# The attention loop of a graph kernel: one bfloat16 product turns both ends' types, GpSimd adds the residual rows, and a square root with a reciprocal stands for a power

## The reference

```python
h = relu(layernorm(x))
k, q, v = per-type projections of h (weights and biases chosen by node type)
k_rot, msg = k[src], v[src] turned by a 16x16 matrix per head and edge type
att = (q[dst] * k_rot).sum(-1) * pri[edge_type] / 4
alpha = softmax of att over the edges of one destination
aggr = segment_sum(msg * alpha, dst)
res = per-type projection of gelu(aggr), blended with h by sigmoid(skip)
x = x + layernorm(res) * ln_g[type] + ln_b[type]
x = x + graph_conv(graph_conv(relu(layernorm(x))))
```

## Time and profile before

| what | value |
|---|---|
| median of 3 runs | 2546.35 us (2545.54 to 2549.22) |
| span of the profiled execution, first to last instruction | 2543.6 us |
| time of that execution itself | not given; the median lies 2.75 us above its span |
| attention loop within the span | about 350 to 1349 us |
| mean granted TensorE clock over the span | 0.793 |
| PE, DVE, ACT, POOL busy over the span | 69%, 77%, 52%, 65% |

### The profile page before, as it was taken

The page is one execution under the profiler, slowest core; times in us unless marked ns, Lnnn a source line. Parts: engine busy times, 40 slices in busy tenths (PEclk is TensorE's granted clock), DMA queues, the critical chain, the costliest instruction groups (busy, mean ns, idle before and its releaser), DMA issues. The chain is left out here.

```text
span 2543.6 us, 48846 instructions
## 1 busy us (share of the span) xinstructions
PE 1755.3 (69%) x12706; PEld 1459.1 (57%) x12706; DVE 1955.8 (77%) x6737; ACT 1311.8 (52%) x3626; POOL 1661.0 (65%) x1791
## 2 busy tenths in 40 slices
PE   3650029999999999999992698995677677770000
PEld 0110019999999999999991466663454445540000
DVE  6999759999999999999996699997555577770000
ACT  5970027777777777777771377775222233320000
POOL 0004658777777777777761377774777677777776
PEclk9995559999999999999996799997555555555555
DMA  7005967777777777777760366664444454441111
GB/s 205 11 0 189 375 200 182 193 194 189 194 192 194 192 192 194 189 192 194 189 178 24 92 181 173 186 178 122 124 134 133 113 110 106 104 90 40 41 40 34
DMA packets 425000, 372.99 MB, mean 147 GB/s; under 512 B 47762, under 2 KB 379390, under 8 KB 421760
## 3 DMA queue, kind: packets, MB, share of 16 engines
q1 hardware_dynamic: 387504, 275.43, 39.1%
q0 software_dynamic: 31360, 64.76, 12.3%
q10 hardware_dynamic: 5886, 29.91, 2.9%
HBM read 226.63 MB, written 146.53 MB: 147 GB/s over the span
## 5 line engine op out<-in xcount | busy, mean ns | idle before, releaser
L812 POOL DMA_INDIRECT att_xsd<-xt,ends_i x392 | 391.8, 999 | 94.7 <-issue 94.2
L995 PE MATMUL att_kvc<-att_hm,w_kv 128*128 128x128 f32 x2352 | 295.0, 275 | 0.0
L1699 DVE TENSOR_TENSOR_SCAN conv_sT<-keep,conv_sT,conv_pT 128x128 f32<-128x128 bf16 x390 | 186.9, 479 | 138.5 <-PE conv_pT L1674 134.4
L1680 PE MATMUL conv_pm<-w,conv_sT 128*128 128x128 f32 x784 | 268.3, 445 | 16.5 <-DVE conv_res L1706 14.6
L995 PEld LDWEIGHTS att_kvc<-att_hm,w_kv 128*128 128x128 f32 x2352 | 278.9, 192 | 0.0
L1674 PE MATMUL conv_pT<-ident,conv_row 128*128 128x128 f32 x392 | 179.8, 459 | 140.9 <-DMA conv_row<-ta,idx 76.6
L1110 DVE TENSOR_TENSOR att_kvm<-att_kvc,att_rel_in 128x1024 f32<-128x1024 f32 x196 | 239.9, 1224 | 2.9 <-issue 1.9
L1623 POOL DMA_INDIRECT conv_row<-t,idx x196 | 187.4, 956 | 69.4 <-issue 57.6
L1628 POOL DMA_INDIRECT out_dram<-conv_res,out_i x196 | 192.7, 983 | 59.7 <-issue 57.9
L1680 PEld LDWEIGHTS conv_pm<-w,conv_sT 128*128 128x128 f32 x784 | 200.1, 315 | 53.3 <-DVE conv_sT L1699 42.9
L1623 POOL DMA_INDIRECT conv_row<-ta,idx x196 | 185.1, 944 | 68.5 <-issue 53.7
(11 more groups left out here) (251 smaller groups left out, 4762.2 us busy)
## 6 DMA issues: line engine op xcount, KB each, us to landing
att_mask_in_t<-type_row SPq DMA_DIRECT2D x196, 192.0 KB
xt<-xr ACTq DMA_DIRECT2D x23, 1224.0 KB, 7.8
att_nxr<-xt SPq DMA_DIRECT2D x97, 262.0 KB
att_rel_in<-rel_row SPq DMA_DIRECT2D x196, 128.0 KB, 3.4
out_dram<-att_not SPq DMA_DIRECT2D x97, 256.0 KB
ta<-att_nhs SPq DMA_DIRECT2D x97, 256.0 KB
xr<-in_x_dram SPq DMA_DIRECT2D x20, 1088.0 KB, 17.0
xd_rows<-att_xsd SPq DMA_DIRECT2D x196, 65.5 KB
```

Of the source, the lines that this page charges most:

```text
L812: pool.indirect_dma_start(out=xsd[:, v, k, :], out_offset=None, in_=xt, in_offset=bass.IndirectOffsetOnAxis(ap=ends_i[:, n, k:k + 1], axis ...
L995: nc.tensor.matmul(kvc[:, e], w_kv[:, t, e], hm[:, w, 0, t], start=e == 0 and t == 0, stop=False)
L1680: nc.tensor.matmul(pm[:, k % 2, 0:D], sT[:, k % R], w[:], start=True, stop=True).then_inc(m_ready, 1)
L1699: dve.tensor_tensor_scan(sT[:, n % R], keep[:, n * P:(n + 1) * P], pT[:, n % 2, 0:P], before, ALU.mult, ALU.add).then_inc(s_ready, 1)
```

## The change

Four edits, all in the attention loop:

- POOL copies the 2 x 9 type columns of a tile to a bfloat16 tile `tcol` (3 buffers) in step `s`, behind the gathers of tile `s`. PE turns them by one bfloat16 product with the identity instead of two float32 transposes, into 18 partitions; ACT's copy, SP's write and the bias products follow this shape (query biases move to rows 9 to 17 of `bias9`).
- POOL adds the input rows to `nx1`, at the end of its step, behind a wait for DVE's second count of `x1_step` in the same step. DVE's add goes; DVE's second moments are taken one step later (`u = s - 6`).
- `nve` and the power on POOL go. ACT takes the square root of variance plus epsilon (`nsd`), in even steps between `qT` and the scaling of `nx1`. DVE's `centre` takes its reciprocal.
- DVE waits for the earlier `bn_aggr` before it overwrites the moments.

```diff
# POOL, step s
+                            if k >= 3:
+                                pool.wait_ge(types_seen, k - 2)
+                            pool.tensor_copy(tcol[:, k % 3], xsd[:, v, :, C_TYPE:C_TYPE + K9]).then_inc(tcol_ready, 1)
                             pool.tensor_copy(ats[:, place_of(k)], xsd[:, v, :, C_SO:C_IDX + 1]).then_inc(ats_ready, 1)
...
-                        c = (s - 2) // 2
-                        if s % 2 == 0 and 0 <= c < NGR + 3:
...
-                            pool.tensor_scalar(nve[:], nmv[b][:, :, :, 1], EPS, None, ALU.add).then_inc(ve_done, 1)
...
-                            pool.tensor_tensor(nrs[b][:], nve[:], mh[:], ALU.pow).then_inc(rs_done, 1)
+                        u = s - 5
+                        if on(u):
+                            g, j0 = u // 2, u % 2 * 2
+                            js = slice(j0, j0 + len(tiles_of(u)))
+                            pool.wait_ge(x1_step, 2 * u + 2)
+                            pool.tensor_tensor(nx1[g % RB][:, js], nx1[g % RB][:, js], nxr[g % RN][:, js, 0:D], ALU.add).then_inc(x1_done, 1)
# SP
-                            sp.dma_start(type_row[n].rearrange("(e t) p -> t e p", e=2), typesT[0:K9:SPLIT, k % 4]).then_inc(trow_out[k % 4], 16)
+                            sp.dma_start(type_row[n], typesT[0:2 * K9:SPLIT, k % 4]).then_inc(trow_out[k % 4], 16)
# ACT
-                            nc.scalar.activation(typesT[0:K9, k % 4], tT[:, 0:2], ACT.Copy).then_inc(types_out, 1)
+                            nc.scalar.activation(typesT[0:2 * K9, k % 4], tT[:, 0], ACT.Copy).then_inc(types_out, 1)
...
+                        c = (s - 2) // 2
+                        if s % 2 == 0 and 0 <= c < NGR + 3:
+                            b = c % 2
+                            if og(c):
+                                act.wait_ge(mv1_done, 2 * c + 2)
+                            if og(c - 3):
+                                act.wait_ge(mv2_done, 2 * (c - 3) + 2)
+                            if c >= 2:
+                                act.wait_ge(rs_done, c - 1)
+                            nc.scalar.activation(nsd[b][:], nmv[b][:, :, :, 1], ACT.Sqrt, bias=eps_c[:]).then_inc(sd_done, 1)
# PE, tile k = s - 2
-                            v = k % RX
-                            pe.wait_ge(got[v], k // RX * 32 + 32)
+                            pe.wait_ge(tcol_ready, k + 1)
...
-                            for e in range(2):
-                                m = nc.tensor.transpose(tT[:, e], xsd[:, v, e, C_TYPE:C_TYPE + K9], ident[:])
-                            m.then_inc(types_seen, 1)
+                            nc.tensor.matmul(tT[:, 0], tcol[:, k % 3].rearrange("p e c -> p (e c)"), identb[:],
+                                             start=True, stop=True).then_inc(types_seen, 1)
# DVE
                     def moments(k, u, of):
+                        if u >= 1:
+                            dve.wait_ge((mv1_done, mv2_done)[k], u)
...
                     def centre(c):
+                        dve.wait_ge(sd_done, c + 1)
...
+                        dve.reciprocal(nrs[b][:], nsd[b][:]).then_inc(rs_done, 1)
...
-                        if on(u):
-                            dve.wait_ge(x1_step, 2 * u + 2)
-                            dve.tensor_tensor(x1, x1, nxr[g % RN][:, js, 0:D], ALU.add).then_inc(x1_done, 1)
...
+                        u = s - 6
                         if on(u):
                             dve.wait_ge(x1_done, u + 1)
                             at_u = moments(1, u, nx1[u // 2 % RB])
```

More of the change, by code:

```diff
@@ L729, in hgt_then_graphconv @@
             hm = lb("hm", [P, 2, 2, TYPES, P], F32)
-            typesT = lb("typesT", [P, 4, 2, P], BF16)
+            tcol = lb("tcol", [P, 3, 2, K9], BF16)
+            typesT = lb("typesT", [P, 4, P], BF16)
             mask_in_t = lb("mask_in_t", [P, RM, 2, TYPES, P], BF16)
@@ L745, in hgt_then_graphconv @@
             nmv = [lb(f"nmv{b}", [P, 2, NJ, 2], F32) for b in range(2)]
-            nve = lb("nve", [P, 2, NJ], F32)
+            nsd = [lb(f"nsd{b}", [P, 2, NJ], F32) for b in range(2)]
             nrs = [lb(f"nrs{b}", [P, 2, NJ], F32) for b in range(2)]
@@ L749, in hgt_then_graphconv @@
             nsc = [lb(f"nsc{b}", [P, NJ], F32) for b in range(2)]
-            mh = lb("mh4", [P, 2, NJ], F32)
+            eps_c = lb("eps_c", [P, 1], F32)
             hT = lp("hT", [P, 4, P], F32)
-            tT = lp("tT", [K9, 4, P], F32)
+            tT = lp("tT", [2 * K9, 4, P], F32)
             kvc = lp("kvc", [P, 4, P], F32)
@@ L766, in hgt_then_graphconv @@
                 ls("h_ready"), ls("ats_ready"), ls("types_seen"), ls("h_seen"), ls("types_out"))
+            tcol_ready, sd_done = ls("tcol_ready"), ls("sd_done")
             hm_ready, proj_ready, kvm_ready, q_ready = ls("hm_ready"), ls("proj_ready"), ls("kvm_ready"), ls("q_ready")
@@ L775, in hgt_then_graphconv @@
             nst_done, mv1_done, mv2_done = ls("nst_done"), ls("mv1_done"), ls("mv2_done")
-            ve_done, rs_done, sc_done, r1_done, r2_done = ls("ve_done"), ls("rs_done"), ls("sc_done"), ls("r1_done"), ls("r2_done")
+            rs_done, sc_done, r1_done, r2_done = ls("rs_done"), ls("sc_done"), ls("r1_done"), ls("r2_done")
             y_done, x1_step, x1_done, nhs_done, not_done = ls("ny_done"), ls("nx1_step"), ls("nx1_done"), ls("nhs_done"), ls("not_done")
@@ L795, in _ @@
                     pool.memset(headw[:], 1.0).then_inc(made, 1)
-                    pool.memset(mh[:], -0.5).then_inc(made, 1)
+                    pool.memset(eps_c[:], EPS).then_inc(made, 1)
                     pool.wait_ge(made, 2)
@@ L807, in _ @@
                                 pool.wait_ge(h_ready, (s - RX) * 2 + 2)
-                                pool.wait_ge(types_seen, s - RX + 1)
+                                pool.wait_ge(tcol_ready, s - RX + 1)
                                 pool.wait_ge(ats_ready, s - RX + 1)
@@ L853, in _ @@
                         sp.dma_start(bias9[SPLIT * t:SPLIT * t + SPLIT, 0:2], bias3[:, 2 * D * t:2 * D * (t + 1)].rearrange("k (a d) -> k a d", a=2)).then_inc(bias_in, 16)
-                        sp.dma_start(bias9[SPLIT * t:SPLIT * t + SPLIT, 2], bias3[:, at:at + D]).then_inc(bias_in, 16)
+                        sp.dma_start(bias9[K9 + SPLIT * t:K9 + SPLIT * t + SPLIT, 2], bias3[:, at:at + D]).then_inc(bias_in, 16)
                     def node_load(g):
@@ L995, in _ @@
                                     nc.tensor.matmul(kvc[:, e], w_kv[:, t, e], hm[:, w, 0, t], start=e == 0 and t == 0, stop=False)
-                            nc.tensor.matmul(qp[:, 0], bias9[:, 2], typesT[:, k % 4, 1], start=False, stop=True)
+                            nc.tensor.matmul(qp[:, 0], bias9[:, 2], typesT[:, k % 4], start=False, stop=True)
                             for e in range(2):
-                                m = nc.tensor.matmul(kvc[:, e], bias9[:, e], typesT[:, k % 4, 0], start=False, stop=e == 1)
+                                m = nc.tensor.matmul(kvc[:, e], bias9[:, e], typesT[:, k % 4], start=False, stop=e == 1)
                             m.then_inc(proj_ready, 1)
@@ L1072, in combine @@
                         if c >= 2:
-                            dve.wait_ge(ve_done, c - 1)
+                            dve.wait_ge(sd_done, c - 1)
                             if k == 0:
@@ L1083, in centre @@
                         b = c % 2
+                        dve.wait_ge(sd_done, c + 1)
+                        if c >= 2:
+                            dve.wait_ge(r1_done, min(c - 1, NGR))
+                            dve.wait_ge(y_done, 2 * min(c - 1, NGR))
+                        if og(c - 5):
+                            dve.wait_ge(r2_done, c - 4)
+                        dve.reciprocal(nrs[b][:], nsd[b][:]).then_inc(rs_done, 1)
                         dve.wait_ge(rs_done, c + 1)
```

## The result

| | before | after |
|---|---|---|
| median of the runs | 2546.57 us | 2688.57 us (2687.57 to 2689.87, 4 runs) |
| ratio | 1 | 1.056, 95% interval 1.054 to 1.057 |
| span of the profiled execution | 2543.6 us | 2686.4 us |
| predicted | | 2623 us, range 2592 to 2667 |

The kernel became slower through the loop that I had named, but by 142 us where I had 77, and above my range. What is asked of the experiments is where the other 66 us come from.

A forecast was written before the change was run, and what follows sets the result against it. PE set the pace at 4.955 us a step; a new two-step loop through PE, DVE and POOL sums to 10.71 us, 5.355 a step. Over 192 steps that loses 77 us: 2623 us, range 2592 to 2667.

The forecast's parts named there:

- The mechanism: Type product, PE, DVE's shift, POOL's add, gathers and cast, type product: 10.71 us per two steps, 77 us lost; chance 0.88.
- the wait for the cast: Sign in the new trace: PE waits for POOL's cast before the type product, around 0.5 us a time.
- A side branch is as long ... a tie; it may add some hundredths: Branch over the rotations to DVE's relation product: 2.43 us after the rotations against 2.41 for the projections' branch.
- `centre` at the durations of before: DVE's stretch with `centre` up to the relation product: 2.00 us as in the old trace, plus 0.23 for the reciprocal.
- The new form saves 0.16 us a step: On PE, one bfloat16 type product at 0.06 us replaces two float32 transposes at 0.22 us.
- PE's 4.79 us: PE's pitch per step if PE alone set the pace after the change, against 4.955 us before.
- POOL's part: In the loop: hop from DVE 0.11, add and gap 0.89, gathers 2.23, cast 0.22, back to PE 0.20 us.
- The last hop: From POOL's cast back to PE: 0.11 us and as much for the weight load, taken as 0.20 us.
- ACT's part: Square root of 8 columns every second step, priced 0.19 us: hidden by 0.3 us, with no extra table load.
- The range: 2592 to 2667 us, from loop lengths of 10.43 to 11.17 us with shorter or longer hops, cast, gathers and add.
- the projections' leg: PE from the type product to the projections' end, 4.42 us, and 0.03 to DVE's relation product.
- the gain comes through: Rival: PE's saving shows in the whole kernel, 32 us faster, 2514 us; chance 0.07.

The follow-up runs named there:

- both cuts: Two runs against the changed kernel: POOL's cast moved ahead of the step's gathers, 2570.1 us; or the residual add given back to DVE, 2571.1 us.
- the dose: Changed kernel plus a second POOL cast of 18 columns in each step, between residual add and gathers: 2703.0 us (ratio 1.061).
- the third buffer: Changed kernel with three buffers instead of two for `prod`, DVE's product of query and key: 2641.9 us (ratio 1.037).
- the loop alone: Changed kernel without POOL's `not_` add, with type weights padded to 128 columns and a third `prod` buffer; loop through POOL kept: 2629.7 us (ratio 1.032).
- the copy: Changed kernel with POOL's `not_` add of the constant row turned into a copy of the same rows: 2658.9 us (ratio 1.044).

## Why the prediction was wrong in size

- **The mechanism** held: the two-step loop from PE over DVE and POOL back to PE. The waits name its links, both cuts open it, and the dose between add and gathers lengthens it. Of its signs, the wait for the cast came in every second step only, with 1.0 to 1.2 us at a time in the mean, and not with 0.5 us in each.
- **"A side branch is as long ... a tie; it may add some hundredths" is the step that failed.** The branch took 5.45 us to L1121 in place of 4.44. I had let DVE's L1142 follow the rotations directly. In the code it also waits for the head sums, because `prod` has two buffers; in the trace of before DVE came so late that this wait hardly showed, but it did. I had read the waits from 500 to 1300 us, where it stands with 1.5 us in 10 times, and it did not enter my sum. From 600 to 1300 us:

```profile
DVE att_prod L1142 <- PE att_attc L1055: 1.2, 8, 0.2
```

  The head sums and the hop are 0.35 us of the 1.01 that this branch was too short.
- **`centre` at the durations of before** was the next term. Its branch took 2.89 us instead of 2.43, as L1101 fell beside POOL's `not_`; L1099 just ahead of it took 0.29 us too, against 0.17 without `not_`. The trace of before has the same 0.71 us as a maximum of the same instruction (L1090), and a median of 0.16; I never asked when the two would meet. The runs with `not_` left out (35 us back) and with the third buffer (47 us) show it from both sides. The two overlap, since the branch over the projections sets a floor: both with wide weights give 59 of the 66 us.
- **"The new form saves 0.16 us a step"** was wrong for the change as made. I priced the product by bfloat16 products with 128 columns of weights. With 18, PE alone needs 5.08 us, slower than before by 0.13. In the loop this was worth 6 to 9 us (wide weights alone; wide weights once `not_` is gone), without the loop 47 (2570.1 against 2523.1). With 128 columns and among the other bfloat16 products PE's 4.79 us came as summed.
- **POOL's part** with its hops was priced 0.28 us too long, which hid a part of the miss. `not_`, the cast, the gathers and L1121 to L1146 came within 0.05 us. The last hop was also added up wrongly: 0.11 and as much again are 0.22, not 0.20; measured, the cast's end to PE is 0.05.
- **ACT's part** was right in its result. No table load came with the square roots: the trace has the one of 1.283 us at L481 and the next only at L1231, behind the loop. The square root took 0.30 us instead of 0.19 and stayed hidden. The reciprocal is not hidden: its 0.18 us, 0.22 to the next instruction, lie in the loop between L1153 and L1121, where the side branch had 0.23. In a kernel in which DVE has its old add as well, the pair costs 5 to 6 us.
- **The range** took its bounds only from durations of legs that I had listed. No bound stood for a leg left out (the head sums, the node types' product) or for DVE held up beside POOL. That the loop alone came so near 5.355 is in part luck: the projections' leg was 0.22 us too short and the cast with its way to PE 0.15 too long.
- Of the rivals, "the gain comes through" is true of a neighbouring kernel: 2515.6 us with the cast ahead of the gathers, wide weights and the product among its like.

What is not settled: why the loop falls into steps of 5.08 and 6.30 us in turn and not into even ones. From 684.14 us on, after a disturbance (below), the type products are 5.41 and 5.40 us apart, and then the alternation returns. `not_` does not drive it: without `not_` the steps are 5.08 and 5.90 us, and in the loop alone 4.90 and 5.83. `centre`, which runs every second step, may; that was not tried. The 30 us of the copy can come from its shorter time, from its single input, or from `centre` no longer meeting it. Why a narrow product costs PE more is open as well.

## What to carry to other kernels

When an edit hangs one engine's work on another's late result, write down every branch that leads there, with all of the waits in the code and not only those that cost something in the old trace: this one cost 1.2 us in 8 waits while DVE came late, and 92.6 us in 71 once DVE came early. Ask of each short operation on the new chain what POOL does at that moment. In a queue executed in order, what other engines need early goes ahead of what waits; here one moved cast was worth 118 us.

## What the hardware showed beside that

With the power gone from POOL's queue, three tiles of the loop, 52 steps apart, show a stall between the two gathers. In the changed kernel's timeline of POOL:

```profile
661.29 0.96 POOL L814 DMA_INDIRECT att_xsd<-xt,ends_i  x1 [1.90 <-issue]
```

Between other pairs of gathers the same gap is 0.30 us. The trace of before has none of these; each of the other 15 traces, all without the power, has three. The excess is 1.6 us each, by estimate 5 of the 2629.7 us of the loop alone. The cause was not tried.
